# A mixture of 64 experts: the "plus one, minimum" of the gate moved to GpSimd, a quarter of every second expert's PSUM evictions moved to VectorE

## The reference, cut to what matters

```python
routing_weights = jax.nn.softmax(x2d @ gate_w, axis=-1)
routing_weights, selected_experts = jax.lax.top_k(routing_weights, TOP_K)   # 8 of 64
routing_weights = routing_weights / jnp.sum(routing_weights, axis=-1, keepdims=True)
...
layer_w0 = jax.lax.ragged_dot(sorted_inputs, gate_k, group_sizes, preferred_element_type=jnp.bfloat16)
layer_w1 = jax.lax.ragged_dot(sorted_inputs, up_k, group_sizes, preferred_element_type=jnp.bfloat16)
intermediate = jax.nn.silu(layer_w0) * layer_w1
expert_out = jax.lax.ragged_dot(intermediate, down_k, group_sizes, preferred_element_type=jnp.bfloat16)
...
out = jnp.einsum('tke,tk->te', unsorted, routing_weights.astype(jnp.float32))
```

## Time and profile before

| | |
|---|---|
| Median of 3 runs | 2533.09 us (2528.65 to 2537.09) |
| The profiled execution | 2537.09 us, span 2535.2 us |
| Busy over the span | PE 81%, DVE 68%, ACT 52%, POOL 17% |
| Busy from 643 to 988 us | DVE 342.78, ACT 304.37, PE 236.25, POOL 50.62 us |
| Share of the span that the stage takes | about 15% |

### The profile page before, as it was taken

How to read it: one execution, slowest core, us unless ns; L and a number is a source line. 1 busy time by engine, 2 the same in 40 slices (tenths; PEclk the granted TensorE clock), 3 DMA queues, 4 the chain that set the end, 5 groups by cost and what they waited for, 6 DMA issues and landing times. The chain is left out here.

```text
span 2535.2 us, 35114 instructions
## 1 busy us (share of the span) xinstructions
PE 2045.8 (81%) x11641; PEld 1329.4 (52%) x11657; DVE 1725.2 (68%) x3778; ACT 1306.5 (52%) x2539; POOL 421.0 (17%) x591
## 2 busy tenths in 40 slices
PE   4999999986676676775877796496999999967978
PEld 3676767664333333552654353364766666633545
DVE  5887888774999998745886783764525253467834
ACT  4666666654898987354333365523433333352641
POOL 1332333321111110102531000201101010110000
PEclk9999999997777866796877698598999999986989
DMA  5000000002111101403301200050000000033000
GB/s 203 1 3 1 3 1 3 1 11 89 44 57 57 57 1 34 140 5 69 67 7 45 74 3 18 22 219 2 1 2 0 2 0 2 1 89 85 20 36 17
DMA packets 60207, 94.55 MB, mean 37 GB/s; under 512 B 9275, under 2 KB 47755, under 8 KB 57463
## 3 DMA queue, kind: packets, MB, share of 16 engines
q1 hardware_dynamic: 56780, 87.81, 11.3%
q0 software_dynamic: 1728, 4.22, 0.7%
q10 hardware_dynamic: 1536, 0.49, 0.1%
HBM read 80.53 MB, written 10.49 MB: 36 GB/s over the span
## 5 line engine op out<-in xcount | busy, mean ns | idle before, releaser
L1235 DVE SCALAR_TENSOR_TENSOR moe_acc<-moee_eo,moe_wsel,moe_acc 128x256 f32<-128x256 bf16 x512 | 226.6, 515 | 0.6
L762 DVE SCALAR_TENSOR_TENSOR l_acc<-l_px,l0w_chan,l_acc 128x253 f32<-128x253 f32 (+2 forms) x288 | 137.7, 478 | 98.2 <-POOL l_acc L730 97.6
L1140 PE MATMUL moee_po<-moee_db,moee_hb 96*128 96x256 bf16 (+1 forms) x768 | 135.8, 345 | 23.5 <-ACT moee_eo L1167 18.5
L1167 ACT CAST moee_eo<-moee_po 128x512 bf16<-128x512 f32 x256 | 133.1, 595 | 38.7 <-PE moee_po L1140 36.8
L1125 PE MATMUL moee_pu<-moe_xb,moee_wb 128*128 128x512 bf16 x192 | 70.8, 508 | 78.8 <-DVE moee_ub L1224 78.8
L1140 PEld LDWEIGHTS moee_po<-moee_db,moee_hb 96*128 96x128 bf16 (+1 forms) x768 | 91.4, 121 | 74.2 <-ACT moee_eo L1167 23.9
L3019 DVE SCALAR_TENSOR_TENSOR l3b_sz<-l3b_sig,l3b_pz 128x256 f32<-128x256 f32 x48 | 20.2, 422 | 144.5 <-ACT l3b_sig L2997 144.5
L351 PE MATMUL ln_pt<-ident,xn 128*128 128x128 f32 x176 | 40.6, 424 | 94.7 <-DVE xn L282 94.7
L1669 ACT ACTIVATE l3xa_ex<-l3xa_pS 128x512 f32<-128x512 f32 x128 | 74.0, 605 | 75.4 <-PE l3xa_pS L1582 71.0
L502 PE MATMUL l_pz<-xT,l0w_w_in 128*128 128x256 f32 x384 | 110.4, 411 | 2.4 <-DVE l_sz L801 2.4
L1669 ACT ACTIVATE l2a_ex<-l2a_pS 128x512 f32<-128x512 f32 x128 | 74.0, 605 | 71.9 <-PE l2a_pS L1582 67.3
(11 more groups left out here) (617 smaller groups left out, 5552.2 us busy)
## 6 DMA issues: line engine op xcount, KB each, us to landing
moe_wf<-in_moe_up SPq DMA_DIRECT2D x48, 256.0 KB, 3.1
l3w_w_in<-in_l_w_in SPq DMA_DIRECT2D x1, 8224.0 KB, 26.4
m1b_bc<-bc_rows SPq DMA_DIRECT2D x16, 512.0 KB, 6.4
l0w_w_in<-in_l_w_in SPq DMA_DIRECT2D x1, 6448.0 KB
moe_df<-in_moe_down SPq DMA_DIRECT2D x48, 128.0 KB, 3.2
l_qs<-parts_q SPq DMA_DIRECT2D x36, 128.0 KB
l0w_w_out<-in_l_w_out SPq DMA_DIRECT2D x1, 3072.0 KB
parts_q<-l_pieces SPq DMA_DIRECT2D x16, 192.0 KB, 2.5
```

The source lines that it names most:

```text
L762: nc.vector.scalar_tensor_tensor(out=a, in0=px[:, 0:S - (L0_CONV - 1 - c)], scalar=w, in1=a, op0=ALU.mult, op1=ALU.add).then_inc(tap_done, 1)
L1140: last = nc.tensor.matmul(po[:, t, :], hb[rows, j % H, t * P:(t + 1) * P], db[rows, j % H, :], start=(n == 0), stop=(n == len(parts) - 1))
L1167: nc.scalar.copy(eo[:, e % 2, 2 * q:2 * q + 2, :], po[:, 2 * q:2 * q + 2, :]).then_inc(o_read, 1)
L1235: last = nc.vector.scalar_tensor_tensor(out=acc[:, t, :], in0=eo[:, e % 2, t, :], scalar=wsel[:, t, e:e + 1], in1=acc[:, t, :], op0=ALU.mu ...
```

## The change

Three things are done in the expert loop.

- The "plus one, minimum" on `ex` moves from DVE to POOL. POOL's order becomes: cast units 0 and 1, zero `acc`, then for each `i`: wait for the Exp of unit `i`, do the operation on `ex`, cast unit `i + 2`.
- Of every even expert, DVE evicts the last quarter of `po`; ACT evicts the other three. Of every odd expert ACT still evicts all four. DVE's eviction stands in its order ahead of the additions of that expert. That makes 32 evictions on DVE and 224 on ACT.
- The semaphore `o_read` is split in two, `o_act` and `o_dve`, and a helper, `wait_evicted`, chooses which one to wait for and what count.

```diff
+            def by_act(e):
+                return 4 if e % 2 else 3
+            def act_until(e):
+                return sum(by_act(i) for i in range(e))
+            def dve_until(e):
+                return 4 * e - act_until(e)
+            def wait_evicted(engine, e, q):
+                if q < by_act(e):
+                    engine.wait_ge(o_act, act_until(e) + q + 1)
+                else:
+                    engine.wait_ge(o_dve, dve_until(e) + q - by_act(e) + 1)
...
 # POOL
                     nc.gpsimd.memset(acc[:, :, :], 0.0).then_inc(zeroed, 1)
-                    for i in range(AHEAD, U):
-                        cast_weights(i)
+                    for i in range(U):
+                        pool.wait_ge(exp_done, i + 1)
+                        nc.gpsimd.tensor_scalar(ex[:, i % 4, :], ex[:, i % 4, :], 1.0, MOE_BIG, ALU.add,
+                                                ALU.min).then_inc(one_plus, 1)
+                        if i + AHEAD < U:
+                            cast_weights(i + AHEAD)
...
 # PE, ahead of the matmuls of a quarter
-                                        pe.wait_ge(o_read, 4 * (e - 1) + q + 1)
+                                        wait_evicted(pe, e - 1, q)
...
 # ACT
-                                for q in range(4):
+                                for q in range(by_act(e)):
                                     act.wait_ge(o_done, 4 * e + q + 1)
                                     nc.scalar.copy(eo[:, e % 2, 2 * q:2 * q + 2, :],
-                                                   po[:, 2 * q:2 * q + 2, :]).then_inc(o_read, 1)
+                                                   po[:, 2 * q:2 * q + 2, :]).then_inc(o_act, 1)
...
 # DVE
-                            dve.wait_ge(exp_done, i + 1)
-                            nc.vector.tensor_scalar(ex[:, i % 4, :], ex[:, i % 4, :], 1.0, MOE_BIG, ALU.add,
-                                                    ALU.min).then_inc(one_plus, 1)
                         if i >= LAG:
                             for e in experts(i - LAG):
+                                for q in range(by_act(e), 4):
+                                    dve.wait_ge(o_done, 4 * e + q + 1)
+                                    if e >= 2:
+                                        dve.wait_ge(used, e - 1)
+                                    nc.vector.tensor_copy(eo[:, e % 2, 2 * q:2 * q + 2, :],
+                                                          po[:, 2 * q:2 * q + 2, :]).then_inc(o_dve, 1)
...
                                 for t in range(NT):
-                                    dve.wait_ge(o_read, 4 * e + t // 2 + 1)
+                                    wait_evicted(dve, e, t // 2)
```

More of the change, by code:

```diff
@@ L1077, in mixture @@
             (cast, g_done, u_done, g_read, u_read, exp_done, one_plus, ln_done, inv_done, gated, h_done,
-             o_done, o_read, used, summed, rounded) = st.sem(
+             o_done, o_act, o_dve, used, summed, rounded) = st.sem(
                 "cast", "g_done", "u_done", "g_read", "u_read", "exp_done", "one_plus", "ln_done",
-                "inv_done", "gated", "h_done", "o_done", "o_read", "used", "summed", "rounded")
+                "inv_done", "gated", "h_done", "o_done", "o_act", "o_dve", "used", "summed", "rounded")
             with st.block() as block:
```

## The result

| | before | changed |
|---|---|---|
| Median | 2528.65 us (7 runs) | 2558.56 us (7 runs) |
| Ratio, 95% interval | 1 | 1.0097 (1.0075 to 1.0119) |
| Profiled execution | 2537.09, span 2535.2 | 2566.79, span 2564.9 |
| The stage, first matmul of the router to the last add into `res` | 377.5 us | 405.0 us |

The ratio is +24.6 us on 2533 (19 to 30). The direction was forecast; the amount, +65 us with a range of +27 to +107, was not. It is 1% of the time, and clear of the noise. Of the profiled execution's +29.7 us, 27.5 lie in the stage.

The account below looks back on a forecast made before the run. The prediction took DVE, busy 99.4% in the expert loop, as the limit. It added 2.0 us of DVE work and 63 of POOL contention: +65, 2602 us against the profiled execution (2598 against the median), range 2560 to 2640.

Parts of the forecast that it names:

- What bounds the kernel: In the expert loop's steady part DVE is busy 99.4%, so the stage's time is the sum of DVE's instructions.
- Parts 1 and 2: DVE loses 48 "plus one, minimum" (20.1 us) and gains 32 evictions (22.1 us): +2.0 us.
- Part 3: ACT loses 32 evictions, 19.0 us, worth nothing because ACT already has 40 us idle and DVE's sum covers it.
- Part 4: POOL's 48 added tensor_scalars delay DVE's two-input work in the expert loop: 63 us, between 30 and 90.
- T: Own time of POOL's new tensor_scalar, taken as 1.9 us (1.04 to 2.60); each meeting costs DVE T - 0.26.
- the lower end: POOL's tensor_scalar takes 1.04 us and costs DVE 0.78 us a meeting, a sum of about +30 us.
- Part 5: POOL's casts move behind its tensor_scalar: no cost, and the casts' own 18.6 us of delay to DVE stay.
- rival A: POOL's tensor_scalar costs DVE nothing, and half the spread casts don't collide: -7 us, 2526; chance 0.06 faster, 0.05 unchanged.
- Part 6: DVE's wait for PE's fourth quarter and PE's wait for DVE's evictions are covered by slack: nothing.
- B: Rival, the lower end: POOL's tensor_scalar takes near 1.04 us, time 2565 us; chance 0.35.
- C: The forecast itself: POOL's tensor_scalar takes 1.5 to 2.6 us, time 2585 to 2625 us; chance 0.44.
- D: Rival: POOL's tensor_scalar above 2.6 us, or DVE waits for the fourth quarter; 2640 us at T = 3; chance 0.10.

Follow-up runs that it names:

- e3: Kernel before with only POOL's cast order changed, cast i+2 after the Exp of unit i: ratio 0.9957, stage 371.8 us.
- e8: Kernel before with no "plus one, minimum" on any engine, plus one as bias of ACT's Ln, minimum left out: ratio 0.9980, stage 371.3 us.
- e13: Kernel before with POOL's casts made to wait until DVE finished the multiplications of unit i-2: ratio 0.9969, stage 372.7 us.
- e9: Changed kernel with POOL's operation on ex replaced by a memset to 2.0, which reads nothing: ratio 0.9929, stage 366.3 us.
- e11: Kernel before with POOL's casts in the changed kernel's order and 16 evictions on DVE: ratio 0.9974, stage 372.6 us.
- e4: Kernel before with the changed cast order, plus a two-operation POOL tensor_scalar on scratch tiles per unit: ratio 1.0121, stage 406.8 us.
- e5: Kernel before with the changed cast order, plus a POOL copy on scratch tiles per unit: ratio 1.0113, stage 406.7 us.
- e7: Changed kernel with only the minimum on POOL, plus one as bias of ACT's Ln: ratio 1.0123, stage 410.0 us.
- e1: Changed kernel with all evictions back on ACT, leaving only the "plus one, minimum" on POOL and its order: ratio 0.9985, stage 375.0 us.
- e6: Kernel before with the changed cast order, plus a POOL memset on a scratch tile per unit: ratio 0.9972, stage 371.5 us.

## Why the prediction was wrong, by its own steps

**What bounds the kernel: right, with a limit that it missed.** DVE is the limit before and after. But ACT and PE in turn need about 371 us of a stage of 377.5, as the stages and waits of e3, e8 and e13 have it. ACT's 40 us of idle time looked like room and seem to be waits inside a loop that is nearly as long as DVE's. It did no harm to a forecast of slower; it would have spoiled any forecast of faster.

**Parts 1 and 2, +2.0 us: right.** Measured 21.7 - 20.1 = +1.6. The row of the same size, 0.691, was the right neighbour for 0.678.

**Part 3, ACT's relief worth nothing: right here,** since DVE stays the limit. Whether it is worth something where DVE is light is open: e9's stage is 5.5 us shorter than e3's with about as much work on DVE, but e11, with half the evictions moved, is no faster than e3.

**Part 4, +63 us: the step that failed.** It had T = 1.9, a price of T - 0.26 = 1.64 and four in five meeting. T is 3.6 to 3.8, outside the 1.0 to 2.6 that the prediction named as its sign of being wrong; the price is 0.76 to 0.77 for a meeting and doesn't depend on T (e4, e5, e7); and 44 of 48 meet. Product: 33.5 us instead of 63. The formula was fitted to two casts, which read one element per element written and compute nothing, so that their own time and their reading time could not be told apart in the earlier trace rows. For the same reason the value of the lower end, 0.78, was right: 1.04 us is what it takes to read 1024 elements and write them (e5's copy), and such a copy holds an addition until 0.27 us after its own end.

The Trainium skill (GPSIMD Engine Reference, 3.1 Elementwise) gives 1.03 cycles per element at 1.2 GHz for bodies of at most two operations. The trace disagrees for this instruction: at that clock 3.62 us are an estimated 4.2 cycles for each of 1024 elements, and one operation (e7's 2.75 us) 3.2. The Trainium skill (SBUF — State Buffer, SBUF: two separate sides) says that who starts first has the shared ports for the whole instruction. That holds for e5's copy and not for the tensor_scalar: in the changed kernel three additions ran at the quiet pace under it. The Trainium skill (SBUF — State Buffer, Who interferes with whom) says that a GpSimd instruction which only writes doesn't contend with a two-input one. The runs agree (e9: 29 such instructions under a memset, none slowed).

**Part 5, "the casts' own 18.6 us of delay stay": failed too.** Instruction by instruction the casts held DVE for 18.4 us before and for 8.2 in the changed kernel, 10.2 less. This is the half of rival A that was real, and A had its size (9.3). With it the sum is 1.6 + 33.5 - 10.2 = 24.9 us; the runs gave 24.6.

**Part 6, no new waits: right.** DVE waited 1.0 us for pu, 0.5 for ACT and never for the fourth quarter.

**The rivals.** A fell: no contention was false. B, the lower end at +32, was nearest in time, and that is luck: its T is wrong by a factor of 3.5, and its price came out right only because the formula was wrong too. C, the forecast, fell. D had the longer T, and by its price of T - 0.26 would have been far off.

## What to carry to other kernels

Before moving work to POOL beside a saturated DVE, price what POOL reads from SBUF and where it lands, not how long POOL takes: DVE's two-input instructions pay for the reads, and only if they run beside them. Where POOL's reads are needed anyway, a semaphore that starts them beside a one-input DVE instruction from PSUM made them free here, with two lines. A part of a change run alone (e1) can look free because its reads fell in such a place. And when the busiest engine is at 99%, look for the next limit before counting a gain: an engine busy 88% can sit in a loop that is only 2% shorter.

## What the runs showed of the hardware that was not expected

- POOL's tensor_scalar on 128x1024 bf16 takes 3.62 us at its shortest with two operations and 2.75 with one, where its copy of the same tile takes 1.04 and a memset 0.95.
- POOL's hold on DVE's additions and multiplications is the same for 1.04 us of POOL (0.77 us a meeting) and for 3.62 us (0.76), and absent for a memset.
- POOL's tensor_scalar holds DVE's one-input bf16 tensor_scalar (0.42 us) at its start and at its end, not between (e4).
- That same DVE instruction is slowed by POOL's memset and by POOL's casts too. In e6 eight of them start 0.48 us into a memset and take 0.75 us. POOL, then DVE:

```profile
792.94 0.95 POOL L1113 MEMSET moee_sd<- 128x1024 bf16 x1 [8.63 <-PE moee_po L1148]
```

```profile
793.42 0.75 DVE L1235 TENSOR_SCALAR moee_ex<-moee_ex 128x1024 bf16<-128x1024 bf16 x1
```
